# State space on one core: exponentials multiplied from their PSUM bank, and low rows made by ScalarE

## The chip, the cores and the metric

One core of a Trainium2 chip runs the whole program, and the metric is the device time of that core in microseconds, over several executions. The core has five engines that take their instructions each from its own queue, in the order in which they were written: TensorE (PE in the rows, its weight loads PEld), VectorE (DVE), ScalarE (ACT), GpSimd (POOL) and SyncE (SP, which starts transfers). Between the engines there are only semaphores: an instruction can be made to wait until a counter has reached a value, and then everything behind it in its queue waits too.

## The reference

A decoder with two layers works on 16 sequences of 256 rows and 256 features: self attention, cross attention, experts, a state space, causal cross attention and a feed-forward with low-rank additions, each with a residual and a row norm behind it. The change concerns the state space alone:

```python
z, xBC, dt = split(x @ in_proj_w.T)              # 512, 768 and 8 columns
xBC = silu(causal_conv(xBC, conv_w) + conv_b)    # 4 taps along the sequence
x_part, B_part, C_part = split(xBC)              # 8 heads of 64, and 128, 128
dt = softplus(dt + dt_bias);  A = -exp(A_log)
def step(state, inp):
    decay = exp(A * dt_t)
    state = state * decay + (x_t * dt_t) * B_t   # per head: 64 x 128
    return state, einsum('bhpn,bn->bhp', state, C_t)
y = scan(step) + x_part * D_full
y = y * silu(z);  y = y * rsqrt(mean(y * y) + EPS) * norm_w
out = y @ out_proj_w.T
```

## The kernel before

Six stages run one after the other in `decoder`; the state space is the function `state_space`. It does not scan. For each batch (one sequence of 256 rows, two blocks of 128) the sum over earlier rows becomes a product of matrices: for each head a matrix of decays, the exponential of sums of `a = A * dt` over a range of rows, times the matrix of `C` times `B` with a triangular mask, times the rows `x * dt`.

The sums of `a` are made by PE (`exponents`, L2516 to L2527): a constant triangle times a moving operand that holds the triangle with each column scaled by `a`, one 128x128 piece a head, 8 heads and 2 blocks. So that it stays exact to single precision the operand exists twice, for the high part of `a` (`rhs_hi`, made on DVE by `high_terms`, L2930) and the low part (`rhs_lo`, made on POOL by `low_terms`, L3127); each is 128x1024 for a block. Six results a batch, numbered `u` 0 to 5 and 128x512 each, alternate between two PSUM banks, `e_ps[0]` for even `u` and `e_ps[1]` for odd `u`. ACT takes the exponential of each into `mat` in SBUF (`decays`, L2670). Then `matrices` (L2827) multiplies in place with the masked product `gm` of L2939, on DVE for `u` 0, 2, 4 and on POOL for 1, 3, 5; PE mixes the rows with the result (`mix`, L2552 to L2554).

Around this the stage has, for each pair of batches, projections on PE (`project`) through the two banks `in_ps` in 11 units, B, C, x0, x1, x2 and dt in the even step, x3 and z0 to z3 in the odd one; ACT makes the first tap of the convolution (`first_tap`, L2689), DVE the other three in place (`taps`, L2893, three instructions a unit); `copy_steps` on ACT (L2658) brings the `dt` rows to SBUF, PE turns them (`turn_steps`, L2495), and `time_steps` on DVE (L2905) adds the bias. `sum_experts` on DVE (L2867 to L2859) adds up the experts' outputs of the batch five ahead, with row moments. `tail_rows` (L2947), `skip_terms` (L2990), `gated` (L3002, the gate product), `residual` (L2971), `row_moments` and `scaled_rows` (L2955, the rows `x * dt`, from a PSUM bank) finish a batch on DVE; `upper_y` and `square_y` (L2746, L2753) on ACT split the result and square it, `split_y` on POOL makes its low part, `output` on PE multiplies with the output weights.

The order is written out by hand: each engine has a loop `for n in STEPS` over 24 steps, of which step `n` works on batch `n` and on the projections of the pair ahead, and the order of the calls in the body is the order of its queue. Even and odd steps have bodies of their own.

## Time and profile before

| | us |
|---|---|
| three runs: lowest, median, highest | 2670.41, 2675.45, 2675.78 |
| profiled execution, its own time | 2671.63 |
| its span, first to last instruction | 2669.9 |
| mean granted clock of TensorE, share of full speed | 0.937 |
| busy over the whole span: PE, DVE, POOL, ACT | 2341.5, 1950.1, 1619.4, 1423.5 |
| first and last gate product of the state space | 1671.66, 2026.97 |

The span is in one core's microseconds from its first instruction. Busy time over the whole span mixes six stages with different limits, so a row of the stage itself says more. A row of the timeline gives the start, the time in us, the engine, the line and the operands, out before in; a number behind x joins instructions that follow each other, and brackets at the end hold the engine's idle time before the row and what ended it.

### The profile page before, as it was taken

Reading aid. Unit: us, or ns where it says so; the run is one execution under the profiler, and the core shown is the slowest. Engines: PE = TensorE matmul, PEld = TensorE weight load, DVE = VectorE, ACT = ScalarE, POOL = GpSimd, SP = SyncE. Lnnn points to the kernel's source line nnn. Section 1 sums busy time; section 2 is a strip of 40 time slices with the busy share of each in tenths; the row PEclk is TensorE's granted clock in tenths of the full one; section 3 lists DMA queues with packets and bytes.
Section 4 is the critical chain, followed back from the end, with each engine's and each line's share of the span. In section 5 each row is a group of like instructions: output and inputs, shape, how many; then the busy total and the mean of one; then the engine's idle time right before and its main releaser. Section 6 shows DMA issues by size and latency. Waiting matters only on the chain. (4 is left out here: it accounts for less than half of the span.)

```text
span 2669.9 us, 63255 instructions
## 1 busy us (share of the span) xinstructions
PE 2341.5 (88%) x23480; PEld 1968.6 (74%) x23480; DVE 1950.1 (73%) x3223; ACT 1423.5 (53%) x2223; POOL 1619.4 (61%) x1937
## 2 busy tenths in 40 slices
PE   5999999997799877998999965988995899987998
PEld 4677777775566656998999964777774666756998
DVE  2677777776589872646888857999984588875776
ACT  2566666664466652335666544655652466653333
POOL 3667666764467751275666656777764587863443
PEclk9899999999899987999999987998996799988999
DMA  8566666551889841146666652111002887841111
GB/s 205 131 159 159 160 145 158 153 120 43 245 216 229 219 111 36 52 138 204 224 228 226 230 175 64 41 48 32 21 13 85 213 225 208 224 105 41 53 54 52
DMA packets 227288, 363.44 MB, mean 136 GB/s; under 512 B 51968, under 2 KB 156416, under 8 KB 219520
## 3 DMA queue, kind: packets, MB, share of 16 engines
q1 hardware_dynamic: 207392, 281.32, 39.7%
q0 software_dynamic: 17376, 78.13, 8.6%
q8 instruction: 143, 2.34, 0.4%
q10 hardware_dynamic: 2304, 1.05, 0.2%
q14 instruction: 73, 0.60, 0.1%
HBM read 231.72 MB, written 133.69 MB: 137 GB/s over the span
## 5 line engine op out<-in xcount | busy, mean ns | idle before, releaser
L1369 ACT ACTIVATE self_probs<-self_score_ps 128x768 f32<-128x768 f32 x256 | 208.7, 815 | 183.9 <-PE self_score_ps L1271 182.0
L1585 POOL TENSOR_SCALAR_AFFINE_SELECT self_probs<-self_probs 128x512 f32<-128x512 f32 x256 | 169.5, 663 | 158.6 <-ACT self_probs L1369 158.6
L1506 DVE TENSOR_REDUCE self_neg_max<-self_max_ps 128x2 f32<-128x256 f32 x256 | 108.1, 422 | 165.1 <-PE self_max_ps L88 165.1
L647 ACT ACTIVATE cross_probs<-cross_score_ps 128x1024 f32<-128x1024 f32 x128 | 131.2, 1025 | 101.6 <-PE cross_score_ps L545 100.0
L745 DVE TENSOR_REDUCE cross_neg_max<-cross_max_ps 128x4 f32<-128x1024 f32 x128 | 154.9, 1212 | 39.1 <-PE cross_max_ps L524 39.0
L1507 DVE TENSOR_REDUCE self_neg_max<-self_max_ps 128x2 f32<-128x512 f32 x256 | 174.5, 682 | 0.0
L2297 POOL TENSOR_TENSOR moee_h_lo<-moee_h,moee_h_hi 128x512 fp32r<-128x512 f32 x78 | 112.5, 1442 | 92.3 <-ACT moee_h_hi L2034 91.6
L739 DVE TENSOR_REDUCE causal_block_max<-causal_max_ps 128x6 f32<-128x768 f32 x128 | 120.9, 946 | 56.4 <-PE causal_max_ps L88 55.9
L3592 POOL TENSOR_TENSOR ffn_g_lo<-ffn_g_full,ffn_g_hi 128x512 fp32r<-128x512 f32 x64 | 82.1, 1283 | 129.2 <-ACT ffn_g_hi L3478 116.9
L2034 ACT ACTIVATE moee_h_hi<-moee_h 128x512 fp32r<-128x512 f32 x110 | 69.6, 632 | 163.2 <-DVE moee_h L2200 163.2
L647 ACT ACTIVATE causal_probs<-causal_score_ps 128x768 f32<-128x768 f32 x128 | 103.6, 809 | 99.2 <-PE causal_score_ps L545 99.0
L79 PE MATMUL moee_g_ps<-moee_x_hi,moee_in_hi 128*128 128x256 f32 x440 | 131.3, 298 | 10.0 <-DVE moee_x_lo L2187 5.8
L1271 PE MATMUL self_score_ps<-self_q_stack,self_k_stack 49*128 49x128 f32 (+1 forms) x1024 | 129.0, 330 | 10.0 <-ACT self_probs L1369 6.4
L2200 DVE TENSOR_TENSOR moee_h<-moee_u_ps,moee_silu 128x512 f32<-128x512 f32 x110 | 75.5, 686 | 82.0 <-PE moee_u_ps L81 77.4
L2240 POOL DMA_INDIRECT x_tiles<-kept_x,moek_slot x64 | 65.8, 1029 | 107.1 <-issue 104.1
L79 PE MATMUL moee_y_ps<-moee_out_hi,moee_h_hi 128*128 128x256 f32 x440 | 125.4, 285 | 0.7 <-DVE moee_out_lo L2152 0.7
L81 PE MATMUL moee_g_ps<-moee_x_hi,moee_in_lo 128*128 128x256 f32 x440 | 125.7, 286 | 0.0
L79 PE MATMUL moee_u_ps<-moee_x_hi,moee_in_hi 128*128 128x256 f32 x440 | 125.7, 286 | 0.0
L80 PE MATMUL moee_g_ps<-moee_x_lo,moee_in_hi 128*128 128x256 f32 x440 | 125.7, 286 | 0.0
L80 PE MATMUL moee_u_ps<-moee_x_lo,moee_in_hi 128*128 128x256 f32 x440 | 125.1, 284 | 0.0
L81 PE MATMUL moee_u_ps<-moee_x_hi,moee_in_lo 128*128 128x256 f32 x440 | 125.1, 284 | 0.0
L81 PE MATMUL moee_y_ps<-moee_out_hi,moee_h_lo 128*128 128x256 f32 x440 | 124.9, 284 | 0.0
(507 smaller groups left out, 9479.9 us busy)
## 6 DMA issues: line engine op xcount, KB each, us to landing
self_q<-self_q_split SPq DMA_DIRECT2D x48, 512.0 KB, 3.5
self_q_raw<-self_q SPq DMA_DIRECT2D x32, 768.0 KB, 8.2
cross_stacks<-cross_qk SPq DMA_DIRECT2D x64, 384.0 KB, 6.4
causal_stacks<-causal_qk SPq DMA_DIRECT2D x64, 384.0 KB, 6.4
moe_y_tiles<-lasting_y_out SPq DMA_DIRECT2D x55, 256.0 KB, 2.5
mid<-lasting_y_out SPq DMA_DIRECT2D x48, 256.0 KB, 2.2
x_tiles<-zeros SPq DMA_DIRECT2D x16, 624.0 KB, 5.5
moee_xT<-x_tiles SPq DMA_DIRECT2D x39, 256.0 KB, 7.3
```

The source lines that it names most:

```text
L79: pe.matmul(out, a[0], b[0], start=start, stop=False, **kw)
L80: pe.matmul(out, a[0], b[1], start=False, stop=False, **kw)
L81: return pe.matmul(out, a[1], b[0], start=False, stop=stop, **kw)
L647: nc.scalar.activation(probs[i // 2][:, a, :, lo:], score_ps[:, :, lo:], ACT.Exp, scale=HD ** -0.5).then_inc(prob_ready, 1)
L739: last = dve.tensor_reduce(block_max[:, :, col % 4, :], bank[:, :, 0:3 * P].rearrange("p a (j t) -> p a j t", t=P), AX.X, ALU.max, negate= ...
L745: last = dve.tensor_reduce(neg_max[p][:, tile, :, col % 4, :], bank[:].rearrange("p a (q k) -> p a q k", q=QT), AX.X, ALU.max, negate=True)
L1271: last = pe.matmul(score_ps[:, ab, j * S + k * P:(j + 1) * S], k_stack[p][rows, tile, k * P:(k + 1) * P], q_stack[rows, 4 * tile + c, k * P:],
L1369: nc.scalar.activation(probs[g % 4][:, a, :, P:], score_ps[:, :, P:], ACT.Exp, scale=HD ** -0.5).then_inc(prob_ready, 1)
L1506: dve.tensor_reduce(neg_max[:, tile, :, c, 0:1], bank[:, :, 0:P], AX.X, ALU.max, negate=True)
L1507: dve.tensor_reduce(neg_max[:, tile, :, c, 1:2], bank[:, :, S:2 * S], AX.X, ALU.max, negate=True).then_inc(max_kept, 1)
L1585: pool.affine_select(diagonal, diagonal, [[0, 2], [0, 2], [1, P]], ALU.is_ge, zero, base=0, channel_multiplier=-1).then_inc(prob_masked, 1)
L2297: pool.tensor_tensor(h_lo[p][f][:].rearrange("p j s -> p (j s)"), h[f][:], h_hi[p][f][:].bitcast(F32).rearrange("p j s -> p (j s)"), ALU.s ...
```

## The change

ACT's exponentials for `u` 0, 2 and 4 are no longer written to `mat` but back into their own bank `e_ps[0]`; DVE's product with `gm` reads them there and writes `mat`. PE therefore may use that bank again only after DVE's product: `exponents` 2 and 4, and the first half of `to_rows`, wait for `low_mat_ready` instead of `decay_ready`. The low rows of the sums' operand, two products of 128x1024 a batch on POOL, become 16 scaled copies of 128x128 on ACT, one for each head and block, with the head's column of `a_lo` as scale. They are made in the step before the one that uses them: in even steps 8 behind the last first tap and 8 behind the split of x, in odd steps all 16 at the end. In DVE's body the product for `u` 0 moves up to right behind `masked_products`; in even steps `u` 2 comes between two units of taps and `sum_experts` moves from the start of the step to behind them; `u` 4 comes ahead of `high_terms` or `mean_squares`.

```diff
@@ exponents, to_rows (tensor)
-                if u >= 2:
+                if u in (2, 4):
+                    pe.wait_ge(low_mat_ready, 3 * n + u // 2)
+                elif u >= 2:
                     pe.wait_ge(decay_ready, 6 * n + u - 1)
...
-                    if b:
-                        pe.wait_ge(decay_ready, 6 * b - 1 + q)
+                    if b and q == 0:
+                        pe.wait_ge(low_mat_ready, 3 * b)
+                    elif b:
+                        pe.wait_ge(decay_ready, 6 * b)
@@ decays, low_terms (scalar)
-                if u == 0 and n:
+                if u == 1 and n:
                     act.wait_ge(ssm_done, 2 * n)
-                nc.scalar.activation(mat[:, u, :, :].rearrange("p h t -> p (h t)"), e_ps[u % 2][:],
-                                     ACT.Exp).then_inc(decay_ready, 1)
+                dst = mat[:, u, :, :].rearrange("p h t -> p (h t)") if u % 2 else e_ps[0][:]
+                nc.scalar.activation(dst, e_ps[u % 2][:], ACT.Exp).then_inc(decay_ready, 1)
...
+            def low_terms(b, q):
+                if q == 0:
+                    act.wait_ge(alo_ready, b // 2 + 1)
+                    if b:
+                        act.wait_ge(e_done, 6 * b)
+                for h in range(NH):
+                    last = nc.scalar.activation(rhs_lo[:, q, h, :], upto, ACT.Identity,
+                                                scale=a_lo[:, b % 2 * QT + q, h:h + 1].bitcast(F32))
+                last.then_inc(rlo_ready, 1)
...
                     first_tap(n, 4)
+                    if n >= 0 and soon:
+                        low_terms(n + 1, 0)
                     if real(n + 4):
                         split_x(n + 4)
+                    if n >= 0 and soon:
+                        low_terms(n + 1, 1)
...
                     if now:
                         square_y(n)
+                    if soon:
+                        low_terms(n + 1, 0)
+                        low_terms(n + 1, 1)
@@ matrices (vector and gpsimd)
-            eng.tensor_tensor(mat[:, u, :, :], mat[:, u, :, :],
+            src = mat[:, u, :, :] if u % 2 else e_ps[0][:].rearrange("p (h t) -> p h t", t=P)
+            if u == 0 and n:
+                eng.wait_ge(ssm_done, 2 * n)
+            eng.tensor_tensor(mat[:, u, :, :], src,
@@ low_terms (gpsimd)
-                pool.tensor_tensor(rhs_lo[:, q, :, :], upto.unsqueeze(1).broadcast_to([P, NH, P]),
-                                   a_lo[:, b % 2 * QT + q, :].bitcast(F32).unsqueeze(2).broadcast_to([P, NH, P]),
-                                   ALU.mult).then_inc(rlo_ready, 1)
```

ACT, from the end of an odd step into the next even one. L2753 squares y, L2689 is the first tap, L2670 an exponential. Before:

```order
L2726 ACTIVATE ssm_zs<-ssm_in_ps 128x512
L2753 ACTIVATE ssm_square<-ssm_yz 128x1024
L2689 ACTIVATE ssm_bc<-ssm_in_ps,ssm_cb,ssm_cw 128x512
L2670 ACT_TABLE_LOAD
L2670 ACTIVATE ssm_mat<-ssm_e_ps 128x512
```

The same place in the changed kernel (L2757 the square, L2773 the low rows, L2693 the tap, L2675 the exponential):

```order
L2730 ACTIVATE ssm_zs<-ssm_in_ps 128x512
L2757 ACTIVATE ssm_square<-ssm_yz 128x1024
L2773 ACTIVATE ssm_rhs_lo<-ssm_triang,ssm_a_lo 128x128 x16
L2693 ACTIVATE ssm_bc<-ssm_in_ps,ssm_cb,ssm_cw 128x512
L2675 ACT_TABLE_LOAD
L2675 ACTIVATE ssm_e_ps<-ssm_e_ps 128x512
```

Sixteen copies now stand between the square and the tap, and the exponential has its bank as output.

DVE at the start of the same even step, from the high rows on. L2867 to L2859 are the sum of experts, L2939 the masked product, L2893 the taps, L2827 the products of the decays, L2947 the tail rows. Before:

```order
L2930 TENSOR_TENSOR ssm_rhs_hi<-ssm_triang,ssm_a_hi 128x1024 x2
L2867 SCALAR_TENSOR_TENSOR ssm_y_shared<-ssm_y_routed,moek_weight,ssm_y_shared 128x256 x2
L2874 SCALAR_TENSOR_TENSOR ssm_x<-ssm_y_routed,moek_weight,ssm_y_shared 128x256 x2
L2855 BN_STATS ssm_c_stats<-ssm_x 128x6 x2
L2857 MEMSET ssm_gate 128x1
L2859 BN_AGGR ssm_c_mv<-ssm_c_stats 128x2 x2
L2939 TENSOR_TENSOR ssm_gm<-ssm_g_ps,ssm_triang 128x384
L2893 SCALAR_TENSOR_TENSOR ssm_bc<-ssm_in_ps,ssm_cw,ssm_bc 128x2x255
...
L2827 TENSOR_TENSOR ssm_mat<-ssm_mat,ssm_gm 128x512 x2
L2947 TENSOR_TENSOR ssm_xdt_tail<-ssm_xdt,ssm_tail 128x512
```

In the changed kernel (L2954 the high rows, L2963 the masked product, L2851 the products, L2917 the taps, L2891 the first row of the sum of experts):

```order
L2954 TENSOR_TENSOR ssm_rhs_hi<-ssm_triang,ssm_a_hi 128x1024 x2
L2963 TENSOR_TENSOR ssm_gm<-ssm_g_ps,ssm_triang 128x384
L2851 TENSOR_TENSOR ssm_mat<-ssm_e_ps,ssm_gm 128x512
L2917 SCALAR_TENSOR_TENSOR ssm_bc<-ssm_in_ps,ssm_cw,ssm_bc 128x2x255
...
L2851 TENSOR_TENSOR ssm_mat<-ssm_e_ps,ssm_gm 128x512
...
L2891 SCALAR_TENSOR_TENSOR ssm_y_shared<-ssm_y_routed,moek_weight,ssm_y_shared 128x256 x2
```

The first product stands right behind the masked product, with the sum of experts and all taps behind it; before, the sum and six instructions of taps stood ahead of it.

## Rows read from the trace of the kernel before

**Rows 1.** windows, state-space stage: length, busy us of PE, PEld, DVE, ACT, POOL, clock, DMA

```profile
1645.00:2030.00 385.00, 337.54 (x2334) 284.88 (x2334) 350.33 (x617) 224.05 (x357) 273.85 (x274) 0.94 0.10 30
```

**Rows 2.** timeline of DVE, gate products of batches 3 to 7, 9, 10: start, us, instruction

```profile
1741.40 1.22 DVE L3002 TENSOR_TENSOR ssm_yz<-ssm_yz,ssm_zs 128x1024 f32<-128x1024 f32 x1
1768.82 1.23 DVE L3002 TENSOR_TENSOR ssm_yz<-ssm_yz,ssm_zs 128x1024 f32<-128x1024 f32 x1
1791.43 1.22 DVE L3002 TENSOR_TENSOR ssm_yz<-ssm_yz,ssm_zs 128x1024 f32<-128x1024 f32 x1
...
1819.95 1.23 DVE L3002 TENSOR_TENSOR ssm_yz<-ssm_yz,ssm_zs 128x1024 f32<-128x1024 f32 x1
1842.93 1.22 DVE L3002 TENSOR_TENSOR ssm_yz<-ssm_yz,ssm_zs 128x1024 f32<-128x1024 f32 x1
...
1893.97 1.22 DVE L3002 TENSOR_TENSOR ssm_yz<-ssm_yz,ssm_zs 128x1024 f32<-128x1024 f32 x1
1919.52 1.22 DVE L3002 TENSOR_TENSOR ssm_yz<-ssm_yz,ssm_zs 128x1024 f32<-128x1024 f32 x1
```

**Rows 3.** timeline of ACT, copies before the steps; line views of L2646, L1446, ns min/median/max

```profile
1616.27 1.70 ACT L2646 ACTIVATE ssm_xs<-ssm_xs,ssm_nw 128x256 f32<-128x256 f32 x4
1618.00 1.06 ACT L2649 ACTIVATE ssm_wo_hi<-ssm_xs 128x1024 fp32r<-128x1024 f32 x1
...
L2646 ACT ACTIVATE ssm_xs<-ssm_xs,ssm_nw x4: 497/498/499, 1616.3 to 1617.5; 128x256 f32<-128x256 f32 x4
...
L1446 ACT ACTIVATE self_k_split<-self_k_full x16: 407/408/418, 22.9 to 550.4; 128x256 fp32r<-128x256 f32 x16
```

**Rows 4.** timeline of ACT, start of step 6 (first tap, table load, first exponential)

```profile
1796.61 0.78 ACT L2689 ACTIVATE ssm_bc<-ssm_in_ps,ssm_cb,ssm_cw 128x512 f32<-128x512 f32 x1
1797.41 1.28 ACT L2670 ACT_TABLE_LOAD   x1
1798.70 0.60 ACT L2670 ACTIVATE ssm_mat<-ssm_e_ps 128x512 f32<-128x512 f32 x1
```

**Rows 5.** timeline of DVE, step 6

```profile
1793.76 3.01 DVE L2930 TENSOR_TENSOR ssm_rhs_hi<-ssm_triang,ssm_a_hi 128x1024 fp32r<-128x1024 f32 x2
...
1799.91 4.51 DVE L2893 SCALAR_TENSOR_TENSOR ssm_bc<-ssm_in_ps,ssm_cw,ssm_bc 128x510 f32<-128x510 f32 x6
1804.34 2.58 DVE L2827 TENSOR_TENSOR ssm_mat<-ssm_mat,ssm_gm 128x512 f32<-128x512 f32 x2
...
1809.41 2.36 DVE L2930 TENSOR_TENSOR ssm_rhs_hi<-ssm_triang,ssm_a_hi 128x1024 fp32r<-128x1024 f32 x2 [0.80 <-PE ssm_e_ps L2527]
```

**Rows 6.** line views of L2955 and L2947 on DVE: duration ns min/median/max

```profile
L2955 DVE TENSOR_TENSOR ssm_xdt<-ssm_e_ps,ssm_dt x32: 656/681/691, 1646.1 to 2011.7; 128x512 f32<-128x512 f32 x32
...
L2947 DVE TENSOR_TENSOR ssm_xdt_tail<-ssm_xdt,ssm_tail x16: 679/686/1772, 1661.0 to 2017.5; 128x512 f32<-128x512 f32 x16
```

**Rows 7.** timelines of DVE and POOL, step 7 (third product, residual; POOL's products)

```profile
1834.49 2.38 DVE L2827 TENSOR_TENSOR ssm_mat<-ssm_mat,ssm_gm 128x512 f32<-128x512 f32 x1
...
1837.54 0.88 DVE L2971 SCALAR_TENSOR_TENSOR lasting_y_out<-ssm_xT_ps,ssm_row_scale,ssm_x 128x256 f32<-128x256 f32 x2 [0.68 <-issue]
...
1833.77 2.53 POOL L2827 TENSOR_TENSOR ssm_mat<-ssm_mat,ssm_gm 128x512 f32<-128x512 f32 x2
```

**Rows 8.** timelines of ACT and DVE, passage from step 6 to step 7

```profile
1820.27 0.78 ACT L2689 ACTIVATE ssm_xs<-ssm_in_ps,ssm_cb,ssm_cw 128x512 f32<-128x512 f32 x1 [7.96 <-PE ssm_in_ps L81]
...
1824.91 0.57 ACT L2658 ACTIVATE ahead_front<-ssm_in_ps 8x512 f32<-8x512 f32 x1
...
1826.03 0.18 DVE L2905 TENSOR_TENSOR ssm_v<-ssm_in_ps,ssm_bias 128x32 f32<-128x32 f32 x1
```

**Rows 9.** timeline of PE, step 6, matmuls of 512 columns after a wait

```profile
1803.89 0.79 PE L2526 MATMUL ssm_e_ps<-ssm_rhs_hi,ssm_one_r 128*128 128x512 f32 x1 [3.72 <-ACT ssm_mat L2670]
...
1808.74 0.63 PE L2527 MATMUL ssm_e_ps<-ssm_rhs_lo,ssm_after 128*128 128x512 f32 x1
...
1810.14 0.39 PE L79 MATMUL ssm_in_ps<-ssm_x_hi,ssm_w_hi 128*128 128x512 f32 x1
```

More of the change, by code:

```diff
@@ L2761, in normalize_y @@
                 last.then_inc(out_ready, 1)
+            def low_terms(b, q):
[7 more added lines that the diff above has]
+                last.then_inc(rlo_ready, 1)
             for n in STEPS:
-                now, late = real(n), real(n - 1)
+                now, late, soon = real(n), real(n - 1), real(n + 1)
                 if n % 2 == 0:
@@ L3010, in _ @@
                 if n % 2 == 0:
+                    if now:
+                        masked_products(n)
+                        matrices(dve, n, 0, low_mat_ready)
+                    taps(n, 0)
+                    if now:
+                        matrices(dve, n, 2, low_mat_ready)
+                    taps(n, 1)
                     if real(n + 5) and n != -2:
@@ L3013, in _ @@
                     if now:
-                        masked_products(n)
-                    taps(n, 0)
-                    taps(n, 1)
+                        tail_rows(n)
                     if now:
-                        matrices(dve, n, 0, low_mat_ready)
-                        matrices(dve, n, 2, low_mat_ready)
-                        tail_rows(n)
+                        matrices(dve, n, 4, low_mat_ready)
                     if n >= 0 and soon:
                         high_terms(n + 1)
-                    if now:
-                        matrices(dve, n, 4, low_mat_ready)
                     taps(n, 2)
@@ L3050, in _ @@
                         masked_products(n)
+                        matrices(dve, n, 0, low_mat_ready)
                     if real(n + 5):
@@ L3053, in _ @@
                     if now:
-                        matrices(dve, n, 0, low_mat_ready)
                         matrices(dve, n, 2, low_mat_ready)
@@ L3057, in _ @@
                     taps(n, 0)
+                    if now:
+                        matrices(dve, n, 4, low_mat_ready)
                     if late:
                         mean_squares(n - 1)
-                    if now:
-                        matrices(dve, n, 4, low_mat_ready)
                     if late:
@@ L3120, in scale_rows @@
                 pool.tensor_tensor(row_scale[:], ms[:], neg_half[:], ALU.pow).then_inc(scale_ready, 1)
-            def low_terms(b, q):
-                if q == 0:
-                    pool.wait_ge(alo_ready, b // 2 + 1)
-                    if b:
-                        pool.wait_ge(e_done, 6 * b)
-                pool.tensor_tensor(rhs_lo[:, q, :, :], upto.unsqueeze(1).broadcast_to([P, NH, P]),
-                                   a_lo[:, b % 2 * QT + q, :].bitcast(F32).unsqueeze(2).broadcast_to([P, NH, P]),
-                                   ALU.mult).then_inc(rlo_ready, 1)
             def split_y(n, half):
@@ L3153, in _ @@
                         scale_rows(n - 1)
-                    if n >= 0 and soon:
-                        low_terms(n + 1, 0)
-                        low_terms(n + 1, 1)
                     if late:
@@ L3174, in _ @@
                         scale_x(n + 5)
-                    if soon:
-                        low_terms(n + 1, 0)
                     if late:
                         scale_y(n - 1)
-                    if soon:
-                        low_terms(n + 1, 1)
                     if real(n + 7):
```

## The prediction

> **What bounds the kernel now.** The change lies in one stage of six, the state space, so the question is what that stage is worth and what ends last in it. I read the windows view of the stage first [rows 1]: 385 us, DVE busy 350.3 of them (91%), PE 337.5, POOL 273.9, ACT 224.1. DVE is the nearest to full, PE next. Then I took one mark for each batch in the timeline of DVE, the gate product of line 3002, and read the distance from mark to mark [rows 2]. Call a step even or odd by the number of its batch. Step 6 takes 28.5 us (1791.43 to 1819.95), step 7 23.0, step 4 27.4 (1741.40 to 1768.82), step 10 25.6; step 8 is like step 6, step 2 like step 4. Last I laid the four engines side by side over steps 6 and 7. DVE's waits there are few and short (0.80 and 0.68 are the longest [rows 5, 7]), so its queue, in the order in which it is written, sets the step, and ACT and POOL are in time. A change that shortens DVE's queue helps only as long as ACT stays in time.
>
> **The change part by part.**
>
> *Low rows to ScalarE.* POOL loses two products a batch and ACT gets 16 scaled copies of 128x128. The trace of before has no such copy. The nearest row is four copies of 128x256 with a scale from a column in 1.70 us, each 0.498 long, so one begins 0.40 after the other [rows 3]. A plain copy of 1024 columns lasts 1.06 us and one of 256 lasts 0.408 [rows 3], 0.85 ns a column, so 128 columns less save 0.11: 0.29 us a copy, 2.4 us for the eight of a block, 4.7 for a batch. That is an estimate. Bounds: no more than the 0.40 of the 256-column row, 6.4 a batch; no less than the plain copy of 256 columns, 0.31 apart by the same overlap of 0.1, less 0.11 for the columns: 0.2, 3.2 a batch. I take 4.7, since only the width differs from the nearest row. The Trainium skill, "VectorE: DVE Perf Modes", section on the TRN2 errata, says that ScalarE pays a fixed cost for every instruction with an SBUF source and advises tiles of at least 512 elements. By that rule 16 small tiles are the wrong shape; the row of 128x256 agrees, 0.18 of the 0.29 is not columns, and by the slope of rows 3 the same 2048 columns in one piece would take 1.7 us instead of 4.7.
>
> *Where they stand in an even step.* What matters is not ACT's load (224 + 16 x 4.7 = 299 us of the stage would still fit) but its order. In an odd step the 16 copies stand between the square of y and the next step's first tap. In step 6 before, that tap begins at 1796.61, the table load follows, and the first exponential runs from 1798.70 to 1799.3 [rows 4]; the copies push it to 1803.4, its end to 1804.0. DVE has its masked product from before, and the next thing in its queue is now the first product with the mask, which needs this exponential. In the order of before the sum of experts and two taps stood ahead of it, which took DVE from the end of the high rows at 1796.8 to 1804.3 [rows 5], and hid the wait. Now DVE idles from about 1797.3 to 1804.1, and all of that work comes after. From the first product to the gate product DVE's queue is, from the rows of step 6 [rows 5 to 7]: three products at 0.6 (1.8), four taps at 2.2 (8.9), the sum of experts 2.7 (1796.8 to 1799.9 less the masked product), tail rows 0.6 undisturbed, high rows 2.3, the residual's pair and the skip terms' two, of its size, 0.8 each (2.4), the mean squares 0.1: 18.8. So the gate product comes at 1804.1 + 18.8 = 1822.9 and the step takes 31.5 us instead of 28.5. PE does not bound it: its mix would begin near 1816, five us before the skip terms want it. Against the steps of rows 2 that is +3.0 in steps 6 and 8 (6.1 in both), +4.1 in 2 and 4 (8.2), +6.0 in step 10, whose POOL disturbs DVE less today. Steps 0, 12 and 14 have shorter queues on both sides; I take 4 each from these three values (12, an estimate). Even steps: +32.
>
> *Exponentials multiplied from their bank.* Three of six exponentials a batch stay in PSUM and DVE multiplies from there. The nearest row is another product with one operand in that bank: 656 to 691 ns in all 32 cases [rows 6]. Today's product from SBUF takes 2.58 for two in step 6 [rows 5] and 2.38 for one in step 7, there beside POOL, which multiplies for 2.53 us on end [rows 7]. So the three products cost 0.6 each: 1.3 less in an even step (2.58 for two), 1.8 less in an odd one. An exponential written to PSUM has no row; I take the 0.60 of the one written to SBUF [rows 4], and a tenth either way would be 0.3 a batch. The bank is held longer: PE's next exponents wait for the product, not for the exponential, 0.7 more each. In an odd step the second product stands behind the sum of experts, so PE's last exponents and with them its output come some 5 us later than now.
>
> *An odd step.* Ahead of step 7 the 16 copies come behind the last tap, which waits for PE until 1820.27; from its end at 1821.0 to the end of the copy of the time steps at 1825.5 pass 4.4 us, half a us of it a wait [rows 8]. In the new order the tap comes some 0.3 later and the copies add 4.7: 1821.3 + 4.0 + 4.7 is 1830.0. PE turns the copy by 1830.5 and DVE's time steps begin at 1830.6. DVE itself would be there at 1822.9 + 6.1 = 1829.0 (today 1819.95 to 1826.03), so it waits 1.6. It regains 1.8 in the third product. The residual, today at 1837.54 [rows 7], then waits for PE's late output until about 1841, and the gate product comes at 1846.1, 23.2 after its even step: +0.2. Four odd steps are like this (1 us); in the first and the last three less other work covers the longer chain through the bank, 1.5 each by the same rows (6, an estimate). Odd steps: +7.
>
> *POOL* loses its two products a batch; at the places where they stood neither DVE nor PE waits for it, so their going brings nothing by itself. *DVE's high rows* get faster in odd steps, 3.01 to 2.36 [rows 5], but now end in the new wait and bring nothing.
>
> *Sum:* 32 + 7 = 39 us, on the profiled execution's own 2671.6: 2711. The three runs of before have a median of 2675.45, 3.8 above it; on that scale 2714. I say 2713.
>
> **The rivals.**
>
> *DVE's relief passes to the end: faster.* DVE saves by the rows 1.3 and up to 1.1 (the tail rows, 1.76 against 0.69 undisturbed) in an even step, 1.8 and 0.65 in an odd one [rows 5 to 7]: 4.8 a pair, some 36 us in 7.5 pairs, giving 2638. It decides if the first exponential after the 16 copies is not late, that is if DVE's first product can begin by 1797.3 plus little: even at 0.2 us a copy it begins at 1802.6. For it speaks that DVE is the fullest engine, against it the order: the work that hid the wait now stands behind it. The Trainium skill, "SBUF — State Buffer", section "Who interferes with whom", says that a VectorE instruction with at most one SBUF input does not contend with GpSimd. By that rule alone the products become short and the step of DVE with them; rows 6 agree on the durations. I give it 0.12.
>
> *Copies as cheap as the lower bound and the odd wait gone.* 1.5 us less in each of 8 even steps and 1.5 in six odd ones, 21 off: +18, 2693. Inside my range, part of the forecast's 0.60.
>
> *PE's clock falls in the new waits: slower still.* After 3.72 us without work PE comes back at the lower of its two levels, 1.2 GHz, with 0.63 us for a matmul of 512 columns that takes 0.39 again by 1810.14 [rows 9]: some 6 us at half speed. In an odd step the wait for the time steps is now some 3.2 us and PE's output then sets the residual: about 2.6 us for 6 or 7 odd steps, and copies at 0.40 instead of 0.295 would add 1.7 to most steps. Together +55 to +65, 2735. I give it 0.23.
>
> *Nothing moves* (the copies find idle time on ACT, the relief is used up by waits): 2675. I give it 0.05.
>
> **How the numbers follow.** Forecast 0.60 at 2713 (2690 to 2725), slower still 0.23 (2725 to 2745), no change 0.05, faster 0.12. A range of 2682 to 2738 leaves out about 2 in 10: the faster case and the far end of the slow one. A measurement of this kernel tells 0.2%, 5 us, from no change. Slower by more than that 0.83, same 0.05, faster 0.12.
>
> **What would show it.** Right: on ACT a row of 16 copies of about 0.39 us, 4.7 in all, ahead of the tap in even steps; DVE idle some 7 us before its first product, ended by the exponential; gate products 31 to 32 us apart in even steps and about 23 in odd ones; products from PSUM all at 0.66 to 0.69. Wrong: even steps of 28 us or less, or copies of 0.2 us or less, or odd steps below 22 us. Then the queue of DVE would be the bound that I take it no longer to be.

## The result, and the profile after

The changed kernel takes **2733.74 us** (median of four runs, 2731.21 to 2740.51), the kernel before 2674.36 beside it: a ratio of 1.023, 95% interval 1.0214 to 1.0246, or some 61 us more by the ratio (59 by the medians). The direction is the forecast one and the time lies in the range, but above the band of the forecast itself (2690 to 2725); the size is not the forecast's (39 us), it is that of the rival in which PE's clock falls (2735).

The state-space stage holds nearly all of it: the span grows from 2669.9 to 2729.5 us, the last of the 16 gate products moves by 58.35, from 2026.97 to 2085.32. The windows view of the stage in the kernel after answers to [rows 1], with the same columns:

```profile
1645.00:2090.00 445.00, 354.54 (x2334) 292.03 (x2334) 321.26 (x617) 297.10 (x613) 198.72 (x241) 0.91 0.08 26
```

DVE works 29 us less than before and POOL 75 less, ACT 73 more. All three changes do what they say, and the stage is longer: no engine is near full any more (PE 80%, DVE 72%), so what counts is who waits for whom. The gate products of batches 3 to 7 in DVE's timeline answer to [rows 2]:

```profile
1753.33 1.22 DVE L3026 TENSOR_TENSOR ssm_yz<-ssm_yz,ssm_zs 128x1024 f32<-128x1024 f32 x1
1785.45 1.23 DVE L3026 TENSOR_TENSOR ssm_yz<-ssm_yz,ssm_zs 128x1024 f32<-128x1024 f32 x1
1808.34 1.22 DVE L3026 TENSOR_TENSOR ssm_yz<-ssm_yz,ssm_zs 128x1024 f32<-128x1024 f32 x1
1840.30 1.22 DVE L3026 TENSOR_TENSOR ssm_yz<-ssm_yz,ssm_zs 128x1024 f32<-128x1024 f32 x1
1863.45 1.22 DVE L3026 TENSOR_TENSOR ssm_yz<-ssm_yz,ssm_zs 128x1024 f32<-128x1024 f32 x1
```

Step 6 takes 31.96 us and step 7 23.15. All steps in us, by the same mark, from one profiled execution of each kernel:

| step | 1 | 2 | 3 | 4 | 5 | 6 | 7 | 8 | 9 | 10 | 11 | 12 | 13 | 14 | 15 |
|---|---|---|---|---|---|---|---|---|---|---|---|---|---|---|---|
| before | 19.7 | 27.4 | 22.6 | 27.4 | 22.6 | 28.5 | 23.0 | 28.4 | 22.6 | 25.6 | 20.6 | 25.0 | 22.7 | 21.2 | 18.0 |
| after | 22.5 | 32.4 | 22.9 | 32.1 | 22.9 | 32.0 | 23.2 | 32.3 | 25.3 | 31.9 | 21.9 | 31.0 | 25.4 | 30.5 | 23.6 |
| longer by | 2.8 | 5.0 | 0.3 | 4.7 | 0.3 | 3.4 | 0.2 | 3.9 | 2.7 | 6.4 | 1.3 | 6.1 | 2.7 | 9.3 | 5.6 |

The start of step 6 in ACT's timeline answers to [rows 4] and shows the new row of copies ahead of the tap, the table load and the exponential:

```profile
1813.61 4.78 ACT L2773 ACTIVATE ssm_rhs_lo<-ssm_triang,ssm_a_lo 128x128 fp32r<-128x128 f32 x16
1818.29 0.77 ACT L2693 ACTIVATE ssm_bc<-ssm_in_ps,ssm_cb,ssm_cw 128x512 f32<-128x512 f32 x1
1819.07 1.28 ACT L2675 ACT_TABLE_LOAD   x1
1820.36 0.58 ACT L2675 ACTIVATE ssm_e_ps<-ssm_e_ps 128x512 f32<-128x512 f32 x1
```

DVE's timeline at the same place (number in brackets: idle time ahead, and what ended it). It waits 1.39 us for PE and then 6.01 for that exponential, where in [rows 5] it went from one piece of work to the next:

```profile
1814.40 0.56 DVE L2963 TENSOR_TENSOR ssm_gm<-ssm_g_ps,ssm_triang 128x384 f32<-128x384 f32 x1 [1.39 <-PE ssm_g_ps L2513]
1820.98 0.69 DVE L2851 TENSOR_TENSOR ssm_mat<-ssm_e_ps,ssm_gm 128x512 f32<-128x512 f32 x1 [6.01 <-ACT ssm_e_ps L2675]
```

The line views of the copies and of the products (duration in ns: min/median/max) answer to [rows 3, 6]:

```profile
L2773 ACT ACTIVATE ssm_rhs_lo<-ssm_triang,ssm_a_lo x256: 385/391/399, 1649.7 to 2053.8; 128x128 fp32r<-128x128 f32 x128
...
L2851 DVE TENSOR_TENSOR ssm_mat<-ssm_e_ps,ssm_gm x48: 656/688/692, 1657.1 to 2072.6; 128x512 f32<-128x512 f32 x48
```

The products from the bank are short in all 48 cases, also beside POOL: the Trainium skill's rule in "SBUF — State Buffer", section "Who interferes with whom" (a VectorE instruction with at most one SBUF input, outside the modes that use both of its ports, is left alone by GpSimd), agrees with the row.

Last, two odd steps of the kernel after that differ by 2.1 us with the same instructions. Windows of steps 7 and 9 (DVE's busy time is the third behind the length, the clock the third column from the end), and PE's turn of the time steps in each with a matmul behind it:

```profile
1840.30:1863.45 23.15, 19.67 (x150) 16.02 (x149) 18.75 (x47) 19.14 (x37) 15.62 (x23) 1.00 0.16 46
1895.73:1921.02 25.29, 20.99 (x148) 17.35 (x147) 21.79 (x48) 19.88 (x39) 15.49 (x23) 0.93 0.11 33
```

```profile
1847.09 0.41 PE L2495 MATMUL ssm_in_ps<-lasting_ident,ahead_front 8*128 8x8 f32 x4 [2.67 <-ACT ahead_front L2662]
...
1903.40 0.43 PE L2495 MATMUL ssm_in_ps<-lasting_ident,ahead_front 8*128 8x8 f32 x4 [3.54 <-ACT ahead_front L2662]
1904.35 0.63 PE L80 MATMUL ssm_in_ps<-ssm_x_lo,ssm_w_hi 128*128 128x512 f32 x1
```

PE waits for the copy of the time steps in both, 2.67 us in step 7 and 3.54 in step 9; after the second it comes back at the lower level (0.63 for 512 columns, as in [rows 9]). The later turn is 0.9 of the 2.1 us. The rest is on DVE, which works 3 us more in step 9. The residual of both steps, and the tail rows of step 9 with POOL's products beside them:

```profile
1858.32 0.88 DVE L2995 SCALAR_TENSOR_TENSOR lasting_y_out<-ssm_xT_ps,ssm_row_scale,ssm_x 128x256 f32<-128x256 f32 x2 [1.36 <-PE ssm_xT_ps L81]
...
1908.64 3.56 DVE L2971 TENSOR_TENSOR ssm_xdt_tail<-ssm_xdt,ssm_tail 128x512 f32<-128x512 f32 x1
...
1915.97 0.88 DVE L2995 SCALAR_TENSOR_TENSOR lasting_y_out<-ssm_xT_ps,ssm_row_scale,ssm_x 128x256 f32<-128x256 f32 x2 [0.89 <-issue]
...
1909.11 2.53 POOL L2851 TENSOR_TENSOR ssm_mat<-ssm_mat,ssm_gm 128x512 f32<-128x512 f32 x2
```

In step 7 the tail rows, which have two SBUF inputs, take 0.68 us, and DVE then waits for PE's output. In step 9 they start 0.9 us later, lie beside POOL's products and take 3.56; DVE no longer waits for PE, whose output ends 19.03 us behind the gate product (17.98 in step 7), and the residual begins at 20.24 (18.02), behind the row scale that POOL makes from DVE's late mean squares. So the lower clock adds 0.1 to 0.2 us to step 9, and the tail rows beside POOL some 1.2 (estimates from these rows).

### The profile page after: what moved, and what is told of

Read it like the earlier page. It is cut to its first block and busy times, and to the rows that moved or that the text cites. A ratio compares the mean times of both kernels' runs of the same rounds, so it can differ in the third digit from the quotient of the medians.

```text
span 2729.5 us, 63479 instructions
## 1 busy us (share of the span) xinstructions
PE 2354.4 (86%) x23480; PEld 1972.3 (72%) x23480; DVE 1921.7 (70%) x3223; ACT 1495.5 (55%) x2479; POOL 1542.6 (57%) x1905
```

## Experiments

The change has three parts: low rows made by ScalarE (**copies**), three exponentials multiplied from their bank (**bank**), and a new order of DVE (**order**: the products ahead of the taps and the sum of experts). The first five runs take them one by one and in pairs; copies and order without the bank were not run. Each ratio is against runs of the kernel before on the same chip; the us are that ratio on 2674.

| run | copies | bank | order | ratio, 95% interval | us over before |
|---|---|---|---|---|---|
| e5_order_only | | | new | 1.0069, 1.0045 to 1.0093 | 18 |
| e4_bank_only | | bank | | 1.0121, 1.0098 to 1.0144 | 32 |
| e1_pool_rows | | bank | new | 1.0053, 1.0034 to 1.0073 | 14 |
| e2_copies_only | ACT | | | 1.0202, 1.0177 to 1.0226 | 54 |
| e3_old_order | ACT | bank | | 1.0299, 1.0277 to 1.0321 | 80 |
| the change | ACT | bank | new | 1.0230, 1.0214 to 1.0246 | 61 |

**Low rows back on POOL.** The copies leave ACT; POOL's two products stand where they stood.

```diff
-                for h in range(NH):
-                    last = nc.scalar.activation(rhs_lo[:, q, h, :], upto, ACT.Identity,
...
+                pool.tensor_tensor(rhs_lo[:, q, :, :], upto.unsqueeze(1).broadcast_to([P, NH, P]),
```

> The changed kernel with its low rows back on POOL, where they stood before; the three products from the bank and the new order of DVE stay. Theory (the 16 copies ahead of the exponential are the price): the first exponential of an even step ends some 5 us earlier, about 8 us after the gate product, DVE's idle before its first product falls from 6 us to about 2, and the odd step's passage loses the 4.7 us too: 2665 us, between 2650 and 2690. Rival (the longer chain through the held bank, the new order and PE's lower clock are the price): even steps stay at 31 us or more, 2710 us or more.

Measured 2693.39 us, just above the band that I gave and 14 over before by the ratio. The copies are 47 of the 61 us. The even steps still take 29.8, since a second wait stands behind the first. DVE's and ACT's timelines in step 6:

```profile
1813.28 0.69 DVE L2834 TENSOR_TENSOR ssm_mat<-ssm_e_ps,ssm_gm 128x512 f32<-128x512 f32 x1 [1.35 <-ACT ssm_e_ps L2675]
...
1818.00 0.69 DVE L2834 TENSOR_TENSOR ssm_mat<-ssm_e_ps,ssm_gm 128x512 f32<-128x512 f32 x1 [1.81 <-ACT ssm_e_ps L2675]
...
1815.92 1.09 ACT L2735 ACTIVATE ssm_x<-ssm_x,ssm_c_shift,ssm_c_rstd 128x256 f32<-128x256 f32 x2 [1.43 <-POOL ssm_c_shift L3110]
1816.91 0.57 ACT L2675 ACTIVATE ssm_mat<-ssm_e_ps 128x512 f32<-128x512 f32 x1
1817.39 0.58 ACT L2675 ACTIVATE ssm_e_ps<-ssm_e_ps 128x512 f32<-128x512 f32 x1
```

The second and third exponential are queued on ACT behind the normalization of x, which waits for POOL. ACT waits there in the old order too (1.74 us in step 6 of the kernel before), but DVE is at its two units of taps meanwhile and comes to the products without a wait; my expectation had not looked there.

**Copies alone, old order.** Undoes bank and order.

```diff
-                dst = mat[:, u, :, :].rearrange("p h t -> p (h t)") if u % 2 else e_ps[0][:]
+                dst = mat[:, u, :, :].rearrange("p h t -> p (h t)")
...
-                        masked_products(n)
-                        matrices(dve, n, 0, low_mat_ready)
-                    taps(n, 0)
+                    if real(n + 5) and n != -2:
+                        sum_experts(n + 5)
+                    if now:
+                        masked_products(n)
+                    taps(n, 0)
```

> The kernel before with one thing changed: the low rows made by ScalarE, where the changed kernel has them. Exponentials go to SBUF and DVE has its old order. Theory: in even steps the sum of experts and two taps, 7 us ahead of the first product, cover the copies, and the step stays at 28.5 us; in odd steps the copies delay the turn of the time steps by 4.5 us and DVE has nothing ahead of them: 7 odd steps of about 27 us, 2705 us, between 2690 and 2715. Rival (the copies find idle time on ScalarE): odd steps stay at 23, 2675 to 2685 us.

2732.01 us, dearer than both theories. The odd steps take 26.3 to 27.8, as expected, but the even ones 29.7 to 30.9 instead of 28.5. DVE's timeline in steps 6 and 7:

```profile
1820.99 1.53 DVE L2910 SCALAR_TENSOR_TENSOR ssm_bc<-ssm_in_ps,ssm_cw,ssm_bc 128x510 f32<-128x510 f32 x2 [2.75 <-ACT ssm_bc L2689]
...
1851.39 0.19 DVE L2922 TENSOR_TENSOR ssm_v<-ssm_in_ps,ssm_bias 128x32 f32<-128x32 f32 x1 [4.11 <-PE ssm_in_ps L2495]
```

The two taps of DVE, which the prediction counted as cover, wait themselves for ACT's first tap, and that stands behind the copies too. Only the sum of experts covers.

**Copies and bank, old order.** The changed kernel with DVE's order of before.

```diff
                 if n % 2 == 0:
+                    if real(n + 5) and n != -2:
+                        sum_experts(n + 5)
                     if now:
                         masked_products(n)
-                        matrices(dve, n, 0, low_mat_ready)
                     taps(n, 0)
```

> The changed kernel with DVE's order of before (sum of experts and two taps ahead of the first product); copies on ScalarE and products from the bank stay. Theory (it is the order that laid the copies bare): even steps 27 to 28 us, since the cover is back and the products are 1.3 us shorter; odd steps keep the late passage, some 25: 2685 us, between 2670 and 2705. Rival (the bank held until the product makes PE's chain late whatever the order): even steps of 31 us and more, 2715 us or more.

2760.98 us, the slowest of all: even steps 31.9, as the rival had them, odd 29.5. The theory falls. The new order did not lay the copies bare; beside the held bank it is worth 18 or 19 us (80 to 61 with the copies, 32 to 14 without).

**Bank alone.**

```diff
-                if u >= 2:
+                if u in (2, 4):
+                    pe.wait_ge(low_mat_ready, 3 * n + u // 2)
+                elif u >= 2:
                     pe.wait_ge(decay_ready, 6 * n + u - 1)
...
-            eng.tensor_tensor(mat[:, u, :, :], mat[:, u, :, :],
+            eng.tensor_tensor(mat[:, u, :, :], src,
```

> The kernel before with one thing changed: three exponentials a batch stay in the bank and DVE multiplies them from there. Low rows on POOL, order of before. Theory (products from the bank are worth 1.3 us in an even and 1.8 in an odd step, on the engine that sets both): even steps 27, odd steps 21.5, 2650 us, between 2640 and 2665. Rival (the bank held longer delays PE's exponents, its mix and its output by as much as DVE gains): 2675 to 2700 us.

2709.61 us: dearer than the rival had it. PE's timeline in step 7 shows why, and DVE's shows who pays:

```profile
1853.27 0.47 PE L2528 MATMUL ssm_e_ps<-ssm_rhs_hi,ssm_one_r 128*128 128x512 f32 x1 [3.68 <-DVE ssm_mat L2834]
...
1853.91 0.63 PE L2528 MATMUL ssm_e_ps<-ssm_rhs_hi,ssm_one_r 128*128 128x512 f32 x1
...
1861.44 0.16 DVE L2969 TENSOR_SCALAR ssm_ms<-ssm_g_ps 128x2 f32<-128x2 f32 x1 [0.82 <-PE ssm_g_ps L2579]
```

In the old order the sum of experts stands ahead of the first product, so PE's next exponents wait 3.68 us for the bank, PE comes back at half speed, and its output is late for DVE's mean squares and residual (waits of 0.82 and 0.75 us). The tail rows of that step take 3.02 us beside POOL (0.69 before), but DVE still waits for PE behind them, so they do not set the step. Odd steps grow from 22.6 to 25.8 in the middle of the stage, with every product short.

**Order alone.**

```diff
-                    if real(n + 5) and n != -2:
-                        sum_experts(n + 5)
                     if now:
                         masked_products(n)
+                        matrices(dve, n, 0, low_mat_ready)
                     taps(n, 0)
+                    if now:
+                        matrices(dve, n, 2, low_mat_ready)
                     taps(n, 1)
-                    if now:
-                        matrices(dve, n, 0, low_mat_ready)
-                        matrices(dve, n, 2, low_mat_ready)
+                    if real(n + 5) and n != -2:
+                        sum_experts(n + 5)
...
```

> The kernel before with one thing changed: DVE's new order (masked product and first product ahead of the taps and the sum of experts). Exponentials to SBUF, low rows on POOL. Theory, after the first four runs (the order opens two waits in even steps, for the table load and first exponential and for the one behind the normalization of x, some 3 us together, and pays for itself only where the bank is held): even steps 30.5 to 31, odd steps 23, 2697 us, between 2688 and 2708. Rival (the new order is better by itself, as it is 17 us better with the bank held): 2665 us or less.

2688.58 us, inside the expected band: in the middle of the stage even steps of 29.5 to 30.6 and odd ones of 22.5 to 22.9. So the order costs 18 us where nothing is held and brings 18 where the bank is. Its step 15 has a lesson of its own, which comes under the hardware.

**The same copies at other places.**

```diff
+                    if n >= 0 and soon:
+                        low_terms(n + 1, 0)
+                        low_terms(n + 1, 1)
                     first_tap(n, 4)
-                    if n >= 0 and soon:
-                        low_terms(n + 1, 0)
...
                     first_tap(n, 1)
+                    if now:
+                        low_terms(n, 1)
```

> The changed kernel with the same 32 copies a pair at other places of ScalarE's queue: all 16 of an odd batch ahead of the last tap of the even step, where ScalarE is idle 8 us; of an even batch the first 8 where they stand, the other 8 behind the second tap. Theory (the place of the copies is the price, not ScalarE's work): odd steps 22 to 22.5, even steps 30 to 30.5, 2710 us, between 2695 and 2720. Rival (the work itself, wherever it stands): 2728 to 2740.

2716.88 us, ratio 1.0168 (1.0142 to 1.0194): 16 us come back for the place alone. By the traces most of them lie in odd steps, above all in steps 9 and 13 (3.2 and 5.4 us); the odd ones in the middle, now 22.1 to 22.4, win 0.6 to 0.8 each. The even steps there do not shorten (31.4 to 33.9). DVE and ACT in step 6:

```profile
1816.87 0.69 DVE L2851 TENSOR_TENSOR ssm_mat<-ssm_e_ps,ssm_gm 128x512 f32<-128x512 f32 x1 [3.68 <-ACT ssm_e_ps L2675]
...
1822.05 0.69 DVE L2851 TENSOR_TENSOR ssm_mat<-ssm_e_ps,ssm_gm 128x512 f32<-128x512 f32 x1 [2.27 <-ACT ssm_e_ps L2675]
...
1817.64 2.43 ACT L2773 ACTIVATE ssm_rhs_lo<-ssm_triang,ssm_a_lo 128x128 fp32r<-128x128 f32 x8
1819.98 1.08 ACT L2735 ACTIVATE ssm_x<-ssm_x,ssm_c_shift,ssm_c_rstd 128x256 f32<-128x256 f32 x2
```

The first wait fell from 6.01 to 3.68, and the copies moved behind the tap made a second one of 2.27: ACT goes from them to the normalization and the next two exponentials without waiting for anyone. PE's next exponents wait 3.25 us for the same copies, but they end at 1820.99, before ACT takes the third exponential at 1821.44, so that wait is hidden.

**Only the third product from the bank.** PE does not want that bank again before the rows of the next batch.

```diff
+                dst = e_ps[0][:] if u == 4 else mat[:, u, :, :].rearrange("p h t -> p (h t)")
...
+            src = e_ps[0][:].rearrange("p (h t) -> p h t", t=P) if u == 4 else mat[:, u, :, :]
```

> The kernel before, and only the third of the three exponentials stays in the bank and is multiplied from there; PE does not want that bank again before the rows of the next batch. Theory (the bank's hold is the price of the other two, since PE wants it back at once): no new wait of PE, the third product of an odd step 0.68 us instead of 2.38, odd steps 1.5 shorter, even steps as before: 2664 us, between 2655 and 2672. Rival (the relief never reaches the end of a step): 2670 to 2685.

2668.23 us beside 2671.21, ratio 0.9994 (0.998 to 1.0008): no difference that can be told. The product is short as expected, and the odd steps win 0.5 us instead of 1.5. Timelines of DVE and POOL in step 7:

```profile
1831.53 0.68 DVE L2831 TENSOR_TENSOR ssm_mat<-ssm_e_ps,ssm_gm 128x512 f32<-128x512 f32 x1
1834.11 0.88 DVE L2975 SCALAR_TENSOR_TENSOR lasting_y_out<-ssm_xT_ps,ssm_row_scale,ssm_x 128x256 f32<-128x256 f32 x2 [1.91 <-issue]
...
1830.80 2.55 POOL L2831 TENSOR_TENSOR ssm_mat<-ssm_mat,ssm_gm 128x512 f32<-128x512 f32 x2
1833.29 0.73 POOL L3124 TENSOR_TENSOR ssm_row_scale<-ssm_ms,ssm_neg_half 128x2 f32<-128x2 f32 x1
```

Of the 1.70 us (2.38 in [rows 7], 0.68 here) 1.2 became waiting: by the code the residual needs the row scale, which stands on POOL behind its own two products and ends at 1834.02. The wait of 0.68 in [rows 7] was the same one, nearly hidden.

**And the odd batches' copies where ACT idles.** The run above, with 16 copies ahead of the last tap of even steps; even batches keep POOL.

```diff
+                    if n >= 0 and soon:
+                        low_terms(n + 1, 0)
+                        low_terms(n + 1, 1)
                     first_tap(n, 4)
```

> The run before of this series (third product alone from the bank) and, in even steps, the 16 copies of the next odd batch on ScalarE ahead of its last tap, where it is idle for 8 us; even batches keep POOL. Theory (copies in an idle stretch cost nothing, and POOL's two products of 1.9 us no longer stand beside DVE's residual and skip terms): within 6 us of the run without them, 2660 us, between 2650 and 2672. Rival (any copy on ScalarE delays the tap and the chain behind it): 2680 or more.

2668.06 us, ratio 0.9993 (0.998 to 1.0006). Half of the copies of the change, put into idle time, cost nothing and bring nothing.

**The even step's waits closed.** The bank and the new order, rows on POOL, and two moves.

```diff
                     if now:
                         masked_products(n)
-                        matrices(dve, n, 0, low_mat_ready)
                     taps(n, 0)
+                    if now:
+                        matrices(dve, n, 0, low_mat_ready)
...
-                    if real(n + 4):
-                        normalize_x(n + 4)
                     if now:
                         decays(n, 1)
                         decays(n, 2)
                         tails(n)
+                    if real(n + 4):
+                        normalize_x(n + 4)
```

> The run with the low rows back on POOL (products from the bank, new order of DVE) and two moves that close the waits its even steps showed: DVE's first tap ahead of its first product, and on ScalarE the normalization of x behind the third exponential instead of ahead of the second. Theory (the even step of that run lost 1.35 us to the table load and 1.81 us to an exponential queued behind a wait for POOL): even steps 26.5 to 27.5, odd steps 22.1, 2660 us, between 2650 and 2675, under the kernel before. Rival (PE, held by the bank, sets the even step as soon as DVE does not wait): even steps 29 or more, 2680 to 2690 us.

2683.20 us, ratio 1.0038 (1.0025 to 1.005), even steps of 28.1 to 29.2 in the middle. The waits of 1.35 and 1.81 are gone (0.73 ahead of the masked product is left), and 1.7 us of 3.2 came back in step 6. DVE's timeline says where the rest is, with POOL's beside it:

```profile
1810.80 2.64 DVE L2875 SCALAR_TENSOR_TENSOR ssm_y_shared<-ssm_y_routed,moek_weight,ssm_y_shared 128x256 f32<-128x256 f32 x2
1813.47 1.78 DVE L2882 SCALAR_TENSOR_TENSOR ssm_x<-ssm_y_routed,moek_weight,ssm_y_shared 128x256 f32<-128x256 f32 x2
...
1811.68 2.89 POOL L2835 TENSOR_TENSOR ssm_mat<-ssm_mat,ssm_gm 128x512 f32<-128x512 f32 x2
```

The sum of experts now stands beside POOL's products, and its two pairs take 2.64 and 1.78 us; in the run with rows on POOL and no further move they take 0.87 and 0.88. The stretch of POOL's work that disturbed the products before disturbs the next instructions with two SBUF inputs. Neither theory had that.

**And nothing held in the last two batches but the third.**

```diff
+        def held(n, u):
+            return u == 4 or u % 2 == 0 and n < B - 2
```

> The run with the waits closed, and in the last two batches, where no tap or projection covers the chain, only the third exponential stays in the bank. Theory (the hold costs the last two steps 5 us each, by step 14 of the bank runs, 26.6 and 23.4, against 21.2 before): 6 us less than the run with the waits closed, between 2 and 11 less. Rival (PE's lower clock sets these two steps, whatever is held): within 2 us of it.

2676.30 us, ratio 1.0010 (0.9997 to 1.0022), 7 us less than the run above, as expected: step 14 falls from 26.6 to 24.3, step 15 from 23.8 to 18.0. By the windows of step 15 the clock goes from 0.64 to 0.91. So hold and clock fall together here. In step 15 the traces part their shares: PE's last pair of exponents begins 7.50 us behind the gate product instead of 8.98, and what follows takes 10.53 us instead of 14.84, with PE's output at full speed. Whether the shorter hold kept the clock up is not shown.

**The same two moves with the copies back on ACT.**

```diff
                     first_tap(n, 4)
+                    if n >= 0 and soon:
+                        low_terms(n + 1, 0)
```

> The changed kernel with the same two moves (tap ahead of the first product, normalization of x behind the third exponential), the copies where the changed kernel has them. Theory (the 4.7 us of copies ahead of the exponential are paid whatever else is closed, in both kinds of step): even steps 30.5 to 31.5, odd steps 23, 2708 us, between 2698 and 2718, some 45 above the same kernel with its rows on POOL. Rival (the copies were dear only because of the second wait behind them): within 25 us of the run with the rows on POOL, 2685 or less.

2730.21 us, ratio 1.0197 (1.0177 to 1.0217): 43 us over the run with rows on POOL by the ratios (47 by the medians), as expected, though both are 20 us above what I gave. With the tap ahead of the product DVE waits for the tap instead:

```profile
1827.90 2.31 DVE L2918 SCALAR_TENSOR_TENSOR ssm_bc<-ssm_in_ps,ssm_cw,ssm_bc 128x510 f32<-128x510 f32 x3 [4.12 <-ACT ssm_bc L2693]
```

**Two wide copies for sixteen.** Same place, same number of elements; the scales of the other seven heads are left out.

```diff
-                for h in range(NH):
-                    last = nc.scalar.activation(rhs_lo[:, q, h, :], upto, ACT.Identity,
-                                                scale=a_lo[:, b % 2 * QT + q, h:h + 1].bitcast(F32))
+                last = nc.scalar.activation(rhs_lo[:, q, :, :], upto.unsqueeze(1).broadcast_to([P, NH, P]), ACT.Identity,
+                                            scale=a_lo[:, b % 2 * QT + q, 0:1].bitcast(F32))
```

> The changed kernel with each block's eight copies of 128x128 replaced by one of 128x1024 with a single scale: all heads get the low part of head 0, so that this part of the computation is changed. The same elements at the same place of the queue. Theory (the price follows the length of the row of copies ahead of the exponential): two copies of some 1.1 us, 2.0 a batch instead of 4.8, so somewhat more than half of the 46 us that the copies cost comes back: 2707 us, between 2695 and 2720. Rival (any row of copies there costs a fixed delay, by PE's clock or by a wait that falls due anyway): 2724 us or more.

2698.16 us, ratio 1.0099 (1.0072 to 1.0125). ACT's timeline at the place where the change has 4.78:

```profile
1806.95 2.19 ACT L2772 ACTIVATE ssm_rhs_lo<-ssm_triang,ssm_a_lo 128x1024 fp32r<-128x1024 f32 x2
```

2.59 us less in each of 16 batches is 41 us of ScalarE's time; 35 come back at the end. Over this stretch the price follows the length of the row of copies, at 0.85 us for each. It is not in proportion: the 2.19 us a batch that are left cost some 12 over the run with rows on POOL (26 against 14, with intervals that just touch), 0.35 for each. In the traces steps 2 to 9 are no longer than in that run (28.9 to 30.0 and 22.1 to 23.1); what is left lies in steps 10 and 12 to 14. The Trainium skill, "VectorE: DVE Perf Modes", section on the TRN2 errata, advises against many small tiles on ScalarE for just this fixed cost, and the two rows agree: 0.30 us of ACT for each 128x128 copy, 1.1 for 128x1024.

No run beats the kernel before by what can be told; the two with the third product alone from the bank stand level with it, and so does the one that holds only the third in the last two batches.

## Why the prediction was right in sign and short in size

**Copies: right.** Forecast 0.39 long, 0.29 apart, 4.7 us a batch; measured 0.391, and 4.78 for 16.

**The even step: right in the middle of the stage.** Forecast for step 6: first product 12.7 us behind the gate product, then a queue of 18.8, in all 31.5. Measured 12.64, 19.32 and 31.96. Steps 2, 4 and 8 are 0.6 to 0.9 over the forecast in the same way: the queue is half a us longer than the undisturbed durations that I summed.

**The odd step: right where nothing new stands beside POOL.** Forecast 23.2 for step 7, measured 23.15; the wait of the time steps, forecast at 1.6, is 1.08, ended by PE's turn, and the residual waits for PE's late output as forecast. Step 9 is the same step with the turn 0.9 us later, the tail rows beside POOL behind it, and 25.29; the sum had no term for those.

**Products from the bank: right by themselves** (0.66 to 0.69 each). **Wrong was the price of the hold.** The prediction put it at 0.7 us for each of PE's next exponents and some 5 us of lateness in odd steps, and let the shorter products pay for it. Alone, the bank costs 32 us (3.68 us of PE's time in one wait, then half the clock). In the new order the first product stands at once behind the mask and the hold is short: from order alone to order and bank the time moves by -4 us, less than the intervals can tell. The sum came out near because prediction and change both had the new order with it.

**Wrong was why the copies are late.** The prediction said that the order before hides them behind the sum of experts and two taps, and that the new order lays them bare. The copies alone in the old order cost 54 us: the taps wait for ACT behind the same copies, and the odd step, where nothing covers the turn of the time steps, pays 4 to 5 us in full. In the new order the copies ahead of step 7 begin 1.9 us before the even step's gate product (1.0 behind it in the old), and DVE waits 1.08 for the turn instead of 4.11. Over the stage the price of the copies is about the same in either order: 54 us alone, 48 beside the bank in the old order, 47 beside it in the new. Going from order alone over bank to the whole, the parts are 18, -4 and 47 us.

**The step of the sum that failed** is the one for the steps without rows of their own: "4 each" for steps 0, 12 and 14 and "1.5 each" for the first and the last three odd ones, taken from the middle steps. Measured: 3.9, 6.1 and 9.3; 2.8, 1.3, 2.7 and 5.6. Steps 12, 14 and 15 alone hold 11.5 us of the 20 that the forecast lacks, steps 9 and 13 another 3.7. In step 14 DVE has no tap and no sum of experts to work off; its three products wait one after the other, 6.74, 1.99 and 1.33 us:

```profile
2043.42 0.69 DVE L2851 TENSOR_TENSOR ssm_mat<-ssm_e_ps,ssm_gm 128x512 f32<-128x512 f32 x1 [6.74 <-ACT ssm_e_ps L2675]
2046.10 0.69 DVE L2851 TENSOR_TENSOR ssm_mat<-ssm_e_ps,ssm_gm 128x512 f32<-128x512 f32 x1 [1.99 <-ACT ssm_e_ps L2675]
```

The chain there is copies, exponential, product, bank, exponents, and PE does it and its whole output at a mean clock of 0.72 (0.92 before); step 15 has 0.71 (0.90 before):

```profile
2031.25:2061.76 30.51, 23.05 (x139) 19.96 (x138) 13.87 (x19) 18.70 (x47) 8.47 (x7) 0.72 0.03 9
2061.76:2085.32 23.56, 17.49 (x104) 14.94 (x102) 10.14 (x26) 6.73 (x12) 9.82 (x14) 0.71 0.04 13
```

PE's last pair of exponents, with its output behind it, parts the longer chain from the clock. Its first matmul in steps 14 and 15, after and then before:

```profile
2046.85 0.80 PE L2528 MATMUL ssm_e_ps<-ssm_rhs_hi,ssm_after 128*128 128x512 f32 x1 [0.54 <-DVE ssm_mat L2851]
...
2070.77 0.80 PE L2528 MATMUL ssm_e_ps<-ssm_rhs_hi,ssm_after 128*128 128x512 f32 x1 [0.54 <-DVE ssm_mat L2851]
```

```profile
1997.30 0.66 PE L2526 MATMUL ssm_e_ps<-ssm_rhs_hi,ssm_after 128*128 128x512 f32 x1 [0.22 <-ACT ssm_mat L2670]
...
2016.56 0.79 PE L2526 MATMUL ssm_e_ps<-ssm_rhs_hi,ssm_after 128*128 128x512 f32 x1
```

From the gate product to that matmul step 14 takes 15.60 us (9.50 before) and step 15 takes 9.01 (7.54): 7.6 us of longer chain. From it to the next gate product they take 14.91 (11.72) and 14.55 (10.41), 7.3 us more with the same work of PE: its output takes 8.7 us in both, 5.65 and 4.76 before. So about half of what these two steps grew by is the lower clock, in these executions. It is not all the change's: order alone has step 15 at 0.70 without a copy or a hold, and of the two runs with the third product alone one has step 14 at 0.79 and 24.2 us, the other at 0.92 and 20.8.

That is the mechanism of the third rival, at other places than it named: not 2.6 us in six odd steps (steps 3, 5 and 7 keep a clock of 1.00, and in step 9 the lower clock adds next to nothing) but at the end. Its time, 2735, is the one measured; its reason covers some 7 of the 20 us that the forecast lacks, so its hit is in part luck.

**DVE's relief** did not pass to the end, as forecast, and the runs show two ways in which it is lost: into a wait for POOL's row scale (third product only), and into the next instruction beside POOL (waits closed, and step 9 of the change itself).

## What to carry to other kernels

Before counting work as cover for a late result, ask of each piece whether it waits for the same engine behind the same delay: two taps counted here as cover and were none. An operand read in place holds its bank until the consumer's turn in its queue comes, so price the hold by what stands ahead of the consumer, not by the consumer's own length. Work for an engine with idle time is free only in the stretch where it idles, and the first and last rounds of a loop need rows of their own, since the work that covers the middle ones is missing there.

## What the hardware showed that was not expected

The same PE instructions with the same waits ran one step at two clocks. Step 15 of the kernel before and of the run with the order alone: windows of the two steps, before first, then PE's timeline of the run with the order alone.

```profile
2009.02:2026.97 17.95, 13.19 (x104) 10.74 (x102) 12.22 (x25) 6.73 (x12) 10.50 (x14) 0.90 0.05 16
```

```profile
2021.40:2043.80 22.40, 17.64 (x104) 15.03 (x102) 12.26 (x25) 7.00 (x12) 10.07 (x14) 0.70 0.04 12
```

```profile
2024.30 0.47 PE L2526 MATMUL ssm_e_ps<-ssm_rhs_hi,ssm_after 128*128 128x512 f32 x1 [2.29 <-DVE ssm_xdt L2955]
...
2027.06 0.77 PE L2526 MATMUL ssm_e_ps<-ssm_rhs_hi,ssm_one_r 128*128 128x512 f32 x1 [1.53 <-ACT ssm_mat L2671]
...
2029.96 0.63 PE L2526 MATMUL ssm_e_ps<-ssm_rhs_hi,ssm_after 128*128 128x512 f32 x1
```

Both steps have these two waits, 2.29 and 1.53 us, and fall to the lower level after the second. In the kernel before the matmul that answers to the last line takes 0.58 us and the next 0.39; here PE stays at the lower level through its whole output, and the step is 4.45 us longer. What decided it the runs don't show, and the hold alone does not: in the 14 traces at hand PE's output of step 15 takes 8.6 to 8.7 us eight times and 4.8 to 5.8 six times, with a run that holds the bank among the short ones (copies and bank in the old order, 5.7) and order alone, which holds nothing, among the long ones. A wait can thus cost nothing or several us by what the clock does behind it, and a step read from one profile can be several us off for that alone.
